# Attention heads turned by DMA transposes in place of TensorE, and every engine's order written anew

## The reference, cut to what matters

```
# block 0: self-attention, cross-attention to ctx, MLP; 16 heads of 16
x = x + attention(LN(x) @ w_qkv + b_qkv, mask_self) @ w_ao + b_ao
x = x + attention(q = LN(x) @ w_q + b_q, kv = ctx @ w_kv + b_kv, mask_cross) @ w_co + b_co
x = x + gelu(LN(x) @ w1 + b1) @ w2 + b2
# block 1: latents = x; keys and values from [ctx, latents], keys of ctx masked; then an MLP
lat = x + attention(q = x @ q_w + q_b, kv = [ctx, x] @ kv_w + kv_b, mask_keys) @ out_w + out_b
out = lat + gelu(rmsnorm(lat) * w @ mlp_w1 + mlp_b1) @ mlp_w2 + mlp_b2
```

## Time and profile before

| | us |
|---|---|
| median of 3 runs (1119.05 to 1125.32) | 1120.4 |
| the profiled execution | 1117.1 |
| its span, first to last instruction | 1115.1 |

### The profile page before, as it was taken

One profiled execution on the slowest core, in us unless ns is written; L12 is line 12 of the kernel. 1 busy time (PEld: TensorE's weight loads), 2 busy tenths in 40 slices (PEclk: granted clock), 3 DMA queues, 4 the chain that ended last, 5 costly groups with the idle time before them and its releaser, 6 DMA issues.

```text
span 1115.1 us, 46381 instructions
## 1 busy us (share of the span) xinstructions
PE 1037.7 (93%) x19304; PEld 908.9 (82%) x19304; DVE 982.0 (88%) x2360; ACT 785.7 (70%) x1773; POOL 633.9 (57%) x903
## 2 busy tenths in 40 slices
PE   6677899999999999999999999999999999999997
PEld 5666678888888888888888888888888888878786
DVE  3888979989989999899999989999999999889774
ACT  2446677877667777777677777766777777666786
POOL 3866666555556565655565656555665566464421
PEclk9898999999999999999999999999999999999999
DMA  9541111122111121221111111111111122110111
GB/s 316 175 146 47 46 28 29 33 43 43 38 34 35 39 37 34 43 43 36 33 38 37 39 34 43 43 33 31 43 33 34 43 43 43 32 28 17 26 30 31
DMA packets 117473, 55.09 MB, mean 49 GB/s; under 512 B 98960, under 2 KB 115088, under 8 KB 116240
## 3 DMA queue, kind: packets, MB, share of 16 engines
q1 hardware_dynamic: 117264, 52.13, 19.4%
HBM read 26.93 MB, written 4.19 MB: 28 GB/s over the span
## 4 chain that ended last, share of the span: by engine, by line
PE 45%; DVE 23%; DMA 12%; ACT 10%; issue 6%; POOL 2%; SPq 1%; ACTq 0%; POOLq 0%; DVEq 0%
PE psum L469 11%; PE psum L649 10%; PE psum L609 7%; PE psum L482 6%; DMA turned_lat<-pair_lat 5%; PE psum L595 5%; DMA turned_cross<-pair_cross 4%; PE psum L576 4%; ACT staging L1867 2%; ACT hid_mlp L1867 2%; DVE prob_self L1214 2%; DVE prob_cross L1243 2%; PE psum L455 2%; DVE mx_ctx L1224 2%; DVE prob_cross L1214 1%
## 5 line engine op out<-in xcount | busy, mean ns | idle before, releaser
L2270 POOL TENSOR_TENSOR prob_self<-prob_self,add_self 128x512 f32<-128x512 f32 x64 | 90.9, 1437 | 87.8 <-DVE prob_self L1214 87.7
L2270 POOL TENSOR_TENSOR prob_cross<-prob_cross,add_cross 128x512 f32<-128x512 f32 x64 | 81.1, 1288 | 59.9 <-DVE prob_cross L1214 59.9
L2219 POOL TENSOR_TENSOR rstd_mlp<-var_mlp,minus_half 128x1 f32<-128x1 f32 x64 | 36.3, 567 | 123.1 <-DVE var_mlp L1137 89.8
L1867 ACT ACTIVATE hid_mlp<-psum,folded,undo_in 128x128 f32<-128x128 f32 x256 | 95.8, 464 | 7.2 <-PE psum L469 7.2
L1867 ACT ACTIVATE staging<-psum,cols,undo_in 128x128 f32<-128x128 f32 x256 | 96.2, 457 | 4.9 <-PE psum L469 3.9
L649 PE MATMUL psum<-hi_n,staging 128*128 128x256 f16 x512 | 94.3, 273 | 1.2 <-DVE staging L1276 1.2
L469 PE MATMUL psum<-turned_mlp,hi_m 128*128 128x128 f16 x1024 | 92.7, 219 | 2.4 <-DMA turned_mlp<-pair_mlp 2.1
L469 PE MATMUL psum<-turned_mlp,hi_n 128*128 128x128 f16 x1024 | 92.5, 219 | 0.3 <-DMA turned_mlp<-pair_mlp 0.3
L649 PE MATMUL psum<-hi_m,parts_mlp 128*128 128x256 f16 x512 | 90.1, 273 | 1.1 <-DVE parts_mlp L1276 1.1
L469 PE MATMUL psum<-turned_mlp,lo_n 128*128 128x128 f16 x512 | 88.9, 219 | 0.0
L469 PE MATMUL psum<-turned_mlp,lo_m 128*128 128x128 f16 x512 | 88.9, 219 | 0.0
(11 more groups left out here) (267 smaller groups left out, 3801.5 us busy)
## 6 DMA issues: line engine op xcount, KB each, us to landing
xin<-in_x SPq DMA_DIRECT2D x32, 128.0 KB, 2.3
late<-in_ctxT SPq DMA_DIRECT2D x4, 1024.0 KB, 7.6
ctxT<-in_ctxT SPq DMA_DIRECT2D x32, 128.0 KB, 2.1
late<-in_x SPq DMA_DIRECT2D x4, 1024.0 KB, 6.2
out<-xb SPq DMA_DIRECT2D x32, 128.0 KB, 1.9
staging<-in_w_m SPq DMA_DIRECT2D x2, 1024.0 KB, 7.2
staging<-in_w_n SPq DMA_DIRECT2D x2, 1024.0 KB, 5.2
mask<-in_mask_cross SPq DMA_DIRECT2D x32, 32.0 KB, 1.9
```

The source lines that it names most:

```text
L1867: last = e.activation(hid[t][g][:, j * P:(j + 1) * P], ps[:, j * P:(j + 1) * P], ACT.Gelu_apprx_tanh, bias=b1[:, 4 * g + j:4 * g + j + 1], ...
L2219: e.tensor_tensor(rstd[t][:, :], var[t][:, :], minus_half[:, :], ALU.pow).then_inc(sem["rstd_" + t], 1)
L2270: e.tensor_tensor(ch, ch, over_heads(a[:, :]), ALU.add).then_inc(sem["added_" + t], 1)
```

## The change

The heads of all three attentions are split in halves before they are turned: ScalarE writes the high half (`heads_high`), VectorE the low half (`heads_low`), both SBUF to SBUF, and SyncE turns the pair with a DMA transpose (`heads_across`). The last projection uses the same six f16 matmuls as the other two; its weights become part of the tile `out`, and its residual is scaled back. The biases of the cross and the latent queries move from VectorE to ScalarE, as two pieces of 128x128 each. The values of ctx and latents get a smaller scale, for which GpSimd computes a few one-time factors. FILL becomes 8: the stages of a unit lie further apart. The lists of all five engines are new; bank numbers too.

```diff
-TOGETHER = {..., "out": {"ao": 0, "co": H}}
+TOGETHER = {..., "out": {"ao": 0, "co": H, "lo": 2 * H}}
-FILL, SLOTS = 6, UNITS
+FILL, SLOTS = 8, UNITS
...
-            def heads_turn(u, t, b):
-                q.wait_ge("constants", IDENT)
-                q.wait_ge("heads_" + t, 2 * u + 2)
-                ps = claim(b, ("heads_turn", t, u), ("headsT_" if t == "lat" else "heads_lo_") + t, u + 1)
-                turned_to(ps, heads[t][:, :]).then_inc(sem["heads_turn_" + t], 1)
...
             def project(u, t, b):
...
+                q.wait_ge("lo_side", 1)
+                q.wait_ge("heads_across_" + t, 16 * (u + 1))
                 ps = claim(b, ("project", t, u), "x_" + t, u + 1)
-                if t == "lat":
-                    for k in range(KH):
-                        last = e.matmul(ps[:, 0:H], headsT[t][:, k, :], w["lo"][:, k, :], start=(k == 0), stop=(k == KH - 1))
-                else:
-                    last = halved_rows(ps, W_OUT[t], 0, h_hi[t], h_lo[t])
+                last = halved_rows(ps, W_OUT[t], 0, h_hi[t], h_lo[t])
...
             def heads_low(u, t):
-                ps = bank[in_bank["heads_turn", t, u]][:, 0:KH * P].rearrange("p (k t) -> p k t", k=KH)
-                q.wait_ge("headsT_" + t, u + 1)
-                e.tensor_tensor(h_lo[t], ps, h_hi[t], ALU.subtract).then_inc(sem["heads_lo_" + t], 1)
+                q.wait_ge("heads_hi_" + t, u + 1)
+                e.tensor_tensor(heads_pair[t][:, 1, :], heads[t][:, :], heads_pair[t][:, 0, :], ALU.subtract).then_inc(sem["heads_lo_" + t], 1)
...
             def add_residual(u, t):
...
-                if t == "lat":
-                    e.tensor_tensor(o[:, :], ps, xb[i][:, :], ALU.add).then_inc(sem["x_" + t], 1)
+                e.scalar_tensor_tensor(o[:, :], ps, undo_of[t], xb[i][:, :], ALU.mult, ALU.add).then_inc(sem["x_" + t], 1)
...
-            def heads_out(u, t):
...
-                e.copy(headsT[t][:, :, :] if t == "lat" else h_hi[t], ps).then_inc(sem["headsT_" + t], 1)
+            def heads_high(u, t):
+                q.wait_ge("heads_" + t, 2 * u + 2)
+                q.wait_ge("heads_across_" + t, 16 * u)
+                e.copy(heads_pair[t][:, 0, :], heads[t][:, :]).then_inc(sem["heads_hi_" + t], 1)
+            def q_bias_cross(u):
...
+                for k in range(KH):
+                    last = e.activation(qT["cross"][:, k, :], ps[:, k * P:(k + 1) * P], ACT.Identity, bias=folded[:, 6 + k:7 + k], scale=down_q[:, 1:2])
+                last.then_inc(sem["q_cross"], 1)
...
+            def heads_across(u, t):
+                q.wait_ge("heads_lo_" + t, u + 1)
+                q.wait_ge("proj_mm_" + t, u)
+                q.wait_ge("heads_across_" + t, 16 * u)
+                e.dma_start_transpose(heads_turned[t][:, :, :, :].rearrange("p i k t -> p (i k) t"),
+                                      heads_pair[t][:, :, :].rearrange("p i h -> p (i h)")).then_inc(sem["heads_across_" + t], 16)
```

```diff
             for t in range(FILL, SLOTS):
                 load_x(t)
+                load_rest(t - 2)
+                across(t - 3, "cross")
+                across(t - 4, "mlp0")
+                across(t - 7, "mlp1")
+                heads_across(t - 6, "lat")
+                store(t - 10)
+                across(t - 1, "self")
+                across(t - 4, "lat")
+                heads_across(t - 2, "self")
+                heads_across(t - 3, "cross")
```

More of the change, by code:

```diff
@@ L853, in _ @@
[L853 to L858 removed]
+            total(0, "qkv", 1)
+            score_bank(0, "self", 2)
+            fold(0, "qkv", 0)
+            fold_rest(0, "qkv", 0)
+            squared_tile(0, "out", 4)
+            squared_tile(0, "side", 4)
+            qk_self(0, 1)
+            fold(0, "q", 4)
@@ new lines, in _ @@
+            score_bank(5, "self", 6)
+            score(5, "self", 2)
+            hidden(1, "mlp0", 0, 0)
+            q_lat(0, 6)
+            hidden(1, "mlp0", 1, 4)
+            score_bank(0, "ctx", 2)
+            score(0, "ctx", 0)
+            k_ctx(1, 6)
+            project(4, "self", 7)
+            k_lat(0, 4)
+            mix(2, "cross", 1)
+            v_lat(0, 7)
+            outward(1, "mlp0", 0, 0)
+            outward(1, "mlp0", 1, 0)
+            q_cross(3, 7)
+            score_bank(0, "lat", 2)
@@ new lines, in _ @@
+            mix(3, "cross", 4)
+            mix(0, "lat", 3)
+            prob_turn_bank(5, "self", 1)
+            score_bank(1, "lat", 4)
+            prob_turn(5, "self", 0)
+            score(1, "lat", 6)
+            v_ctx(1, 2)
+            hidden(2, "mlp0", 0, 3)
+            hidden(2, "mlp0", 1, 0)
+            project(3, "cross", 1)
+            k_ctx(2, 5)
+            v_lat(1, 7)
+            project(0, "lat", 3)
+            k_cross(4, 1)
+            outward(2, "mlp0", 0, 3)
+            prob_turn_bank(1, "ctx", 0)
@@ new lines, in _ @@
+            outward(2, "mlp0", 1, 3)
+            prob_turn_bank(1, "lat", 7)
+            prob_turn(1, "lat", 6)
+            prob_turn(1, "ctx", 4)
+            q_cross(4, 3)
+            v_ctx(2, 5)
+            score_bank(4, "cross", 2)
+            score(4, "cross", 0)
+            hidden(3, "mlp0", 0, 7)
+            hidden(3, "mlp0", 1, 3)
+            hidden(0, "mlp1", 0, 4)
+            mix(1, "lat", 1)
+            q_lat(2, 2)
+            mix(5, "self", 3)
+            score_bank(2, "ctx", 0)
@@ new lines, in _ @@
+            prob_turn(UNITS - 6, "lat", 5)
+            prob_turn(UNITS - 6, "ctx", 4)
+            q_lat(UNITS - 5, 2)
+            project(UNITS - 3, "self", 6)
+            k_cross(UNITS - 3, 3)
+            project(UNITS - 4, "cross", 6)
+            outward(UNITS - 8, "mlp1", 0, 5)
+            mix(UNITS - 6, "lat", 1)
+            score_bank(UNITS - 5, "ctx", 6)
+            score(UNITS - 5, "ctx", 2)
+            outward(UNITS - 8, "mlp1", 1, 5)
+            v_lat(UNITS - 5, 4)
+            k_lat(UNITS - 5, 1)
@@ new lines, in _ @@
+            denominators(5, "self")
+            divided(5, "self")
+            masked(2, "ctx", 0)
+            hidden_lo(3, "mlp0", 1)
+            masked(2, "ctx", 1)
+            heads_low(5, "self")
+            k_spread(2, "lat", 0)
+            largest_score(4, "cross", 1)
+            heads_low(1, "lat")
+            k_spread(2, "lat", 1)
+            low_pair(6, "self")
+            shifted(4, "cross", 1)
+            largest_score(2, "ctx", 0)
+            largest_score(2, "ctx", 1)
```

2078 lines of the change are left out of this document (1155 added, 923 removed).

## The result

The changed kernel took **1088.8 us** at the median (1088.6 to 1089.0), the kernel before beside it 1120.3: a ratio of 0.971 (95% interval 0.968 to 0.974). The forecast was 1085 in 1066 to 1110. The profiled execution took 1088.6 us with a span of 1086.8, 28.5 less than the profiled 1117.1 of before.

The account below looks back on a forecast made before the run. TensorE was taken to set the 31.95 us slot, VectorE 0.7 us behind. From 1117.1, 25.0 slots at 1.35 saved (33.8) and +2.0 outside the steady part gave 1085.3, forecast 1085, range 1066 to 1110.

Parts of the forecast that it names:

- TensorE leads, transposes and f32 projection go: TensorE sets the pace; 0.81 us of transposes and 0.22 of projection leave each slot, 1.03 together, floor 30.96 to 29.93.
- VectorE level with TensorE at 30.1: VectorE's floor goes from 30.27 to 29.90 to 31.04 us a slot, taken as 30.1 with 0.2 for stretched heads_low.
- a sign of being wrong: On VectorE: heads_low standing near 794 ns would show the forecast wrong; 412 to 600 at the median was expected.
- Slot 30.6: Loop slot in the steady part falls from 31.95 to 30.6 us, saving 1.35 in each of 25.0 slots.
- The half us over the higher floor: TensorE and VectorE, now level, hand each other lateness, so the slot stands half a us over the higher floor.
- Outside the steady part +2.0: Fill and drain: -3.5 us of TensorE work, +3 for first-unit landings, +2.5 for the last unit's heads; deeper pipeline 0.
- ScalarE at nothing: ScalarE's query bias pieces and slower copies, 25.8 of 30.6 us a slot busy, cost nothing on the path.
- SyncE and landings at nothing: Eight DMA transposes a unit for five hold SyncE 9.5 us a slot; landings of 2.5, at most 4.6, are covered.
- Late landings: Rival: TensorE waits 0.58 us ahead of each of three projections, slot 32.66, 1137 us; chance 0.10.
- Lost in order: Rival: fill and drain of the deeper pipeline and ScalarE's place in the query path cost 1 us a slot, 1117; chance 0.10.
- VectorE becomes the bound: Rival: all three heads_low stretch to the 794 ns median, VectorE's floor 31.04, slot 31.3, 1103 us; chance 0.20.
- The waits for landings: TensorE's 0.99 idle us a slot, nearly all waiting for two turned inputs, was not let vanish with the new order.

Follow-up runs that it names:

- a_turns: Changed kernel with two 128x128 f32 transposes on TensorE put ahead of every projection: 1102.0 us, 0.9858 of the kernel before.
- b_turns_twice: Kernel before with every TensorE transpose of the heads done twice into the same bank: 1137.8 us, 1.0176 of the kernel before.
- a_q_dve: Changed kernel with the cross and latent query biases back on VectorE inside the loop: 1095.3 us, 0.9793 of the kernel before.
- a_qself_early: Changed kernel with self's query bias on ScalarE behind the normalization of cross, both self key spreads first on VectorE: 1089.5 us, 0.9736 of the kernel before.
- b_q_act: Kernel before with only the cross and latent query biases moved from VectorE to ScalarE inside the loop: 1139.8 us, ratio 1.0183.
- a_qself_act: Changed kernel with self's query bias also on ScalarE, behind the normalization of mlp0: 1103.5 us, 0.9871 of the kernel before.
- a_low_later: Changed kernel with the low half of the cross heads moved on VectorE behind the two latent shifts: 1093.9 us, 0.9780 of the kernel before.
- b_later_q: Kernel before with the latent and cross queries moved later in TensorE's loop, behind other work: 1134.7 us, 1.0139 of the kernel before.

## Why the prediction was right, and where its steps were off

- **TensorE leads, transposes and f32 projection go: right.** Forecast some 32 us less busy, measured 33.6, which is 1.05 for each of the 32 units against 1.03 forecast. (In the 800 us alone it is 30.96 - 29.68 = 1.28 a slot; the 0.2 between is not traced.) The three sets took 0.77 a slot and not 0.81, since the cross set takes 0.23. a_turns and b_turns_twice show that such work counts, in the old order in full (0.59 of 0.60 us a slot), in the new in part (0.43 of 0.72).
- **VectorE level with TensorE at 30.1: right in kind, 0.2 short.** Its floor is 30.33. I took 0.2 a slot for the stretching of the new heads_low. Its cross part alone costs 0.47 at the median (884 against 415), which the prediction had named as a sign of being wrong; the other two cost nothing. And the contention did not stay with the new instruction: the subtraction of self went from 414 to 617 ns at the median and one maximum in two from 0.16 to 0.68, in GpSimd's rearranged loop, while the subtraction of mlp went from 794 to 426. These four together would be 0.8 a slot. VectorE is busy 29.67 against the 29.53 - 0.37 = 29.16 without any new stretching, 0.51 more; the rest is not traced. The step that failed is to price only the added instruction, by a row whose neighbours belong to the old order.
- **Slot 30.6: 0.25 too low**, 25.0 x 0.25 = 6.3 us. The half us over the higher floor came out (30.85 - 30.33 = 0.52), the floor under it did not. That half us is luck: in a_q_dve VectorE got 0.78 more and the slot rose by 0.21, in a_qself_early it got 0.39 less and the slot stayed, so the slot does not stand at a fixed distance over this floor. The sum of the two engines' work had no term for what does set it, the maximum stretched ahead of the latent shifts.
- **Outside the steady part +2.0: measured** -28.5 + 25.0 x 1.10 = **-1.0** by the chain's slots, 3 us too dear. (By ScalarE's, 32.03 and 30.84, it is +1.2: the term is known to some 2 us.) The longer way of the last unit's heads is there, 2.47 us of landing of the latent heads in the last chain at 1062.93, but it and the deeper pipeline cost about what TensorE saves outside. This miss and the one before it have opposite signs, and that the sum came within 3.5 us is in part their doing.
- **ScalarE at nothing: right for this order, wrong as a rule.** It is busy 653.61 / 25.93 = 25.2 a slot, forecast 25.8 at most. But what hid the biases was their place: in b_q_act the same pieces cost 20 us, in a_qself_act one more cost 15. My reason, spare time, did not hold; what counts is the place of each piece in ScalarE's list, which the forecast named as a risk and did not work out.
- **SyncE and landings at nothing: right.** The self heads land in 2.5 at the median, 4.2 at most, as their row of the changed kernel shows (issue on SyncE, ns; under it, us to landing), and TensorE waited for the turned heads nowhere in 300 to 900. The cover of the cross heads, which the prediction did not work out, is thin, as a_low_later showed.

```profile
L2780 SPq DMA_TRANSPOSE heads_turned_self<-heads_pair_self x32: 1188/1198/1816, 41.3 to 985.8; - x32
...
DMA to landing us min/median/max: 2.4/2.5/4.2
```

- **The rivals.** "Late landings" did not come, though in a_low_later a delay of 1.3 to 2 us was enough to bring it in 7 slots. "Lost in order" did not come. "VectorE becomes the bound" came in part: one stretch of VectorE sets the slot, not its total, and the stretching is 0.51 us a slot where it was priced at 1.14: one of the three subtractions, and a maximum and another subtraction that it did not name. So its 1103 was not reached.
- **The waits for landings.** I read 0.99 idle us of TensorE as lateness beside the work, most of which I let stay. b_later_q and b_turns_twice speak for a loop through several engines: it grew with added work, and when covered it came back on VectorE. That the old order's 0.9 went may be a share of the 12 us that the work does not explain; no run tells how much.

## What to carry to other kernels

Where several engines are nearly always busy (here 92, 91 and 78% of the span) and each follows a written list, look for the one hand-over that each slot waits for and shorten what stands just before it; 0.39 us taken off the same engine elsewhere gave nothing, 0.5 us taken off there gave all of it. Before adding or pricing a VectorE instruction with two SBUF inputs, look at what GpSimd does beside it, the small instructions above all: a line moved in GpSimd's list gave 12 us, two moves 16 to 18. And a change of engine for one step is worth what its new place in the list makes it: the same two biases were worth 6 us in lists made for them and cost 20 in lists that were not.

## What the runs showed of the hardware that was not expected

- A 128x8 VectorE maximum with two SBUF inputs lasted up to 690 ns beside a GpSimd addition of 0.9 us, and ended 0.01 to 0.03 us after it in all 20 slots of 300 to 900, and 178 at most without it.
- With eight transposing DMAs in a slot for five, each still held SyncE's queue for 1.19 to 1.21 us at the median, and of the six kinds with a landing in the trace five landed in 2.4 to 2.5 us at the median as before; the turned latents went from 2.5 to 3.3. The DMA share of the steady part went from 0.18 to 0.25 without a new wait.
- Idle time of the leading engine took none of the added work: of 0.60 us a slot put on TensorE in the kernel before, 0.59 came through though it idled 0.99.
